# Last layer of a graph network: where a tile's second normalisation stands in VectorE's instruction order

## The reference

```python
def _L0_gnn_ref(...):
    h = x @ W_in + b_in
    for l in range(4):
        h_scaled = h * dinv
        msg = segment_sum(h_scaled[cols], rows) * dinv
        global_ctx = mean(h, axis=0) @ Wg[l] + bg[l]
        z = relu((h + msg) @ Wl[l] + bl[l] + global_ctx)
        mu, var = mean(z, -1), var(z, -1)
        h = (z - mu) * rsqrt(var + EPS) * gamma[l] + beta[l]
    return h

x = x + _L0_gnn_ref(_layernorm(x), src, dst, ...)
x = x + _L0_ffn_ref(_layernorm(x)[None], ...)[0]
```

## Time and profile before

| | |
|---|---|
| three runs, us | 3340.70, 3347.49, 3347.59 (median 3347.49) |
| span of the profiled execution, us | 3340.5 (the page gives no other time for it) |
| TensorE matmul busy | 3129.2 us, 94% |
| TensorE weight load busy | 1810.2 us, 54% |
| VectorE busy | 1989.9 us, 60% |
| ScalarE busy | 850.9 us, 25% |
| GpSimd busy | 70.6 us, 2% |
| products at line 1342 | 9604, 2143.0 us busy |

### The profile page before, as it was taken

The page is one execution under the profiler, slowest core; times in us unless marked ns, Lnnn a source line. Parts: engine busy times, 40 slices in busy tenths (PEclk is TensorE's granted clock), DMA queues, the critical chain, the costliest instruction groups (busy, mean ns, idle before and its releaser), DMA issues.

```text
span 3340.5 us, 56169 instructions
## 1 busy us (share of the span) xinstructions
PE 3129.2 (94%) x17421; PEld 1810.2 (54%) x17421; DVE 1989.9 (60%) x5304; ACT 850.9 (25%) x1934; POOL 70.6 (2%) x168
## 2 busy tenths in 40 slices
PE   6888898699999999999999999999999999979998
PEld 4666676344444444444444444444444444458887
DVE  7999999755455445545554555455555555545554
ACT  3777787411111111111111111111111111123222
POOL 0000000000000000000000000000000000000100
PEclk8999999799999999999999999999999999989999
DMA  4222212412222222221222222221222222110000
GB/s 133 79 79 79 71 49 79 115 68 75 69 67 70 74 68 67 68 76 67 67 76 69 67 67 73 72 67 67 77 78 69 76 78 74 62 34 19 17 17 19
DMA packets 134136, 225.44 MB, mean 67 GB/s; under 512 B 12277, under 2 KB 106596, under 8 KB 134018
## 3 DMA queue, kind: packets, MB, share of 16 engines
q1 hardware_dynamic: 131666, 217.53, 20.2%
q0 software_dynamic: 2352, 6.40, 0.7%
HBM read 178.17 MB, written 45.74 MB: 67 GB/s over the span
## 4 chain that ended last, share of the span: by engine, by line
PE 80%; DVE 11%; issue 4%; ACT 2%; DVEq 1%; DMA 1%; SPq 0%; ACTq 0%; POOL 0%; POOLq 0%
PE bank L1342 50%; PE bank L1212 9%; PE bank L1416 5%; PE bank L1422 5%; PE bank L1300 4%; PE bank L1230 2%; PE bank L1198 2%; PE bank L1290 2%; PE bank L1228 1%; PE bank L1236 1%; DMA tab<-in_x 1%; DVE region L865 1%; DVE region L858 1%; DVE st L870 1%; DVE region L878 1%
## 5 line engine op out<-in xcount | busy, mean ns | idle before, releaser
L1342 PE MATMUL bank<-tab,region 128*128 128x512 f16 x9604 | 2143.0, 379 | 11.4 <-DMA region<-adjacency 11.2
L1342 PEld LDWEIGHTS bank<-tab,region 128*128 128x128 fp8e4 x9604 | 940.3, 98 | 1063.0 <-DVE tab L790 17.1
L1212 PE MATMUL bank<-region 128*128 128x320 bf16 x1862 | 316.4, 320 | 49.8 <-DVE region L670 48.3
L670 DVE TENSOR_SCALAR region<-iota_w,src_col,src_w 128x640 bf16<-128x640 int16 x931 | 361.0, 437 | 0.0
L865 DVE SCALAR_TENSOR_TENSOR region<-bank,c_back,bias 128x256 f32<-128x256 f32 x196 | 94.8, 483 | 405.7 <-PE bank L1300 405.7
L1029 ACT ACTIVATE tab<-region 128x640 fp8e4<-128x640 uint8 x490 | 307.2, 712 | 18.5 <-DVE region L701 18.5
L1212 PEld LDWEIGHTS bank<-region 128*128 128x128 f16 x1862 | 232.6, 144 | 124.4 <-DVE region L670 95.7
L1127 ACT ACTIVATE sd<-mv,eps_c 128x1 f32<-128x1 f32 x196 | 57.8, 295 | 820.8 <-DVE mv L872 820.8
L862 DVE TENSOR_TENSOR region<-bank,region 128x256 f16<-128x256 f32 x196 | 83.2, 425 | 297.6 <-ACT region L1125 297.6
L1125 ACT ACTIVATE region<-bank 128x256 f16<-128x256 f32 x196 | 75.3, 384 | 594.9 <-PE bank L1290 594.9
L1416 PE MATMUL bank<-tab 128*128 128x384 f32 (+1 forms) x544 | 177.2, 484 | 2.6 <-DMA b_s<-in_L_ffn_b 2.6
(11 more groups left out here) (194 smaller groups left out, 2143.9 us busy)
## 6 DMA issues: line engine op xcount, KB each, us to landing
region<-adjacency SPq DMA_DIRECT2D x196, 784.0 KB, 4.3
adjacency<-tab SPq DMA_DIRECT2D x12, 3136.0 KB, 13.9
region<-in_x POOLq DMA_DIRECT2D x48, 128.0 KB, 2.3
out<-region SPq DMA_DIRECT2D x48, 128.0 KB, 1.7
tab<-in_x SPq DMA_DIRECT2D x1, 6016.0 KB
tab<-in_L_ffn_W SPq DMA_DIRECT2D x4, 512.0 KB, 4.2
Wg_s<-in_L_gnn_Wg SPq DMA_DIRECT2D x1, 1024.0 KB
region<-in_L_gnn_Wl SPq DMA_DIRECT2D x1, 1024.0 KB, 5.6
```

What stands on the lines that cost most here:

```text
L670: ins = v.tensor_scalar(hot_s[:, j, :], iota_w[:], src_col[:, ds(start + j, 1)], src_w[:, ds(start + j, 1)], ALU.is_equal, ALU.mult)
L1212: ins = mm(bank[k % 2 * 2 + half][:, 0:HALF], hot_d[:, :, j], hot_s[:, j, half * HALF:(half + 1) * HALF], start=j == 0, stop=j == WIN - 1)
L1342: ins = mm(acc[a][:, :], A_s[:, a, m, :], tab[:, here + m, :], start=m == 0, stop=m == T - 1)
```

## The change

Two helpers are cut out of the last layer's tile on VectorE, `moments(t)` (lines 892 to 897 of the kernel before) and `normal(t)` (lines 898 to 905), and one on ScalarE, `spread(t)` (lines 1131 and 1132). For each of the 48 tiles of the loop in the last layer, `moments` of the tile before now stands between `U` and the split, `normal` of the tile before between the split and the wait for the weight product, and on ScalarE `spread` of the tile before between the copy of the transpose and the square root of the layer's own normalisation. For the last tile all three stand behind the loop. `normal` writes its product to `Zg` instead of `Z`. The other layers are unchanged.

```diff
+            def moments(t):
+                end_own.at(t * CE)
+                hold(dve, x1_ready, t + RING + 1)
+                end_own.done(v.bn_stats(st[:], H[:, t, :]))
+                end_own.hold()
+                end_own.done(v.bn_aggr(mv2[:], st[:]))
+                end_own.wait()
+                v.tensor_copy(mv_all[:, t, :], mv2[:]).then_inc(var2_ready, 1)
+
+            def normal(t):
+                end_own.at(t * CE + 2)
+                dve.wait_ge(std2_ready, t + 1)
+                end_own.done(v.reciprocal(rstd_all[:, ds(t, 1)], sd2[:]))
+                end_own.wait()
+                end_own.done(v.tensor_scalar(Zg, H[:, t, :], mv_all[:, t, 0:1], rstd_all[:, ds(t, 1)],
+                                             ALU.subtract, ALU.mult))
+                end_own.wait()
+                add_rows(t, Zg).then_inc(xsum, 1)
...
+                    late = last and a < RING
+                    if late:
+                        moments(t - 1)
                     dve.wait_ge(uT_copied, n + 2)
                     v.tensor_tensor(uT[:, 1, :, :], T3[3], uT[:, 0, :, :], ALU.subtract).then_inc(uT_split, 1)
+                    if late:
+                        normal(t - 1)
 
                     dve.wait_ge(mm_done, n + 1)
...
                     v.tensor_tensor(H[:, t, :], hf, xb[:, u, :], ALU.add).then_inc(x1_ready, 1)
-                    hold(dve, x1_ready, t + RING + 1)
-                    end_own.done(v.bn_stats(st[:], H[:, t, :]))
...
-                    add_rows(t, Z).then_inc(xsum, 1)
                 tiles(dve, step, n0)
+                if last:
+                    moments(T - 1)
+                    normal(T - 1)
...
+            def spread(t):
+                act.wait_ge(var2_ready, t + 1)
+                a.activation(sd2[:], mv_all[:, t, 1:2], ACT.Sqrt, bias=eps_c[:]).then_inc(std2_ready, 1)
...
                     a.activation(uT[:, 0, :, :], T3[3], ACT.Copy).then_inc(uT_copied, 1)
+                    if last and s < RING:
+                        spread(t - 1)
                     act.wait_ge(var_ready, n + 1)
                     a.activation(sd[:], mv[:, 1:2], ACT.Sqrt, bias=eps_c[:]).then_inc(std_ready, 1)
...
-                        act.wait_ge(var2_ready, t + 1)
-                        a.activation(sd2[:], mv_all[:, t, 1:2], ACT.Sqrt, bias=eps_c[:]).then_inc(std2_ready, 1)
```

More of the change, by code:

```diff
@@ L886, in step @@
                         return
-                    end_own.at(t * CE)
                     u = (a + 1) % RING if a < RING else 0
@@ L1129, in step @@
                         high(n, there + t, hf, n + T, h_ready, hi_ready)
-                    else:
-                        act.wait_ge(var2_ready, t + 1)
-                        a.activation(sd2[:], mv_all[:, t, 1:2], ACT.Sqrt, bias=eps_c[:]).then_inc(std2_ready, 1)
                 tiles(act, step, n0)
+                if last:
+                    spread(T - 1)
             layers(act, one)
```

## The result

| | before | after |
|---|---|---|
| runs, median us | 3344.59 (3340.70 to 3347.59, 4 runs) | 3295.55 (3291.18 to 3299.39, 4 runs) |
| ratio, 95% interval | | 0.9858 (0.9846 to 0.9870) |
| profiled execution: span, time | 3340.5 | 3297.5, 3299.24 |

What follows compares the result with a forecast made beforehand. The prediction took a loop through VectorE and TensorE to bound the last layer at 12.46 us a tile, against TensorE's 11.45. Gains of 47.5 + 1.4 = 48.9 us gave 3347.5 - 48.9 = 3298.6 us, range 3289 to 3311.

Steps and rivals of the forecast that it cites:

- The circle of 12.35 to 12.46 us: Last layer's loop through VectorE and TensorE, line 865 to `U` to weight product, said to set the pace per tile.
- with 1.8 us to spare: Last layer: with 2.84 us moved out, the loop falls to 9.6 us, below TensorE's own 11.45 us.
- Moments hidden between `U` and split, scaling behind it: Last layer's VectorE gaps: moved steps of 1.14 and 1.22 us cost 0, leaving 0.6 and 0.5 us.
- Cadence or idle rows: Last layer's 47 periods: gain taken as 47.5 us from transpose starts, not 37.4 us from TensorE's idle.
- The rival with 0.06: Last layer: only TensorE's shown idle comes back, gain 38.8 us, time 3308.7 us; chance 0.06.
- the missing 0.2 us: Per tile of the last layer, the difference between the gain by transpose starts and by TensorE's idle rows.
- The last tile: Behind the last layer's loop: `U` and the final transpose come sooner, gain 1.4 us, bounds 1.0 and 1.5.
- the 1.27 us worked out: Last tile: `U` ends 1.27 us earlier, by layer 2's 1.94 us from the start of ScalarE's copy.
- the last tile's own residual steps: Behind the last tile: these steps stand there as before, so their change was put at 0.
- From span to median: Whole kernel: the median's 7.0 us above the profiled span was carried over, from 3291.6 to 3298.6 us.

Runs made afterwards that it cites:

- e2: Kernel before with the transpose after 20 sums instead of 14 and the weight product after 30 instead of 24; 3352.9 us.
- e3: Kernel before with six sums instead of ten between the transpose and the weight product, VectorE's and ScalarE's lists untouched; 3299.4 us.
- e6: Changed kernel with eight unused 128x256 adds on VectorE per tile of the last layer, right behind the residual; 3333.8 us.
- e7: Changed kernel with moments, scaling and row sum all between `U` and the split; 3310.5 us.
- e1: Kernel before with only scaling and row sum moved behind the next tile's split, moments and square root left at the tile's end; 3292.3 us.
- e4: Changed kernel with moments, scaling and row sum all behind the split, none between `U` and the split; 3294.1 us.
- e9: Changed kernel with unused TensorE products: 8 ahead of the row sum, 22 ahead of the weights' spread, 12 ahead of the first expert weights; 3294.6 us.
- e8: Changed kernel with unused TensorE products: 26 ahead of the row sum, 20 ahead of the expert weights' spread; 3295.9 us.

## Why the prediction was right

*What bounds the last layer.* The circle of 12.35 to 12.46 us held in every test: not moved by giving `U` more time (e2), shortened as computed on the other arc (e3), lengthened by more work (e6, where 12.5 to 13.1 us were expected and 12.23 came, since the eight adds took 2.68 us and not 2.8 to 3.4, and the loop without them is 9.55 us).

*After the change TensorE is the bound, with 1.8 us to spare.* Cadence 11.449 us, predicted 11.45. The reserve is 11.45 - 9.55 = 1.9 us by e6.

*Moments hidden between `U` and split, scaling behind it.* Both as computed, with more left over than I had said: 0.77 and 0.94 us where I gave 0.6 and 0.5. Two causes: VectorE begins the moments at 2630.69, before `U`'s instruction has ended (2630.77), and the square root is back before it is asked for.

*Cadence or idle rows.* I took 47.5 us against the 37.4 us of the idle rows, and 47.5 us came. The rival with 0.06 would have been 3308.7. The reason that the prediction gave for the missing 0.2 us, a transpose that begins before the sums in front of it are marked as ended, is right for 0.16 of it: e3 and e7 lose 0.17 and 0.34 us a tile where the idle rows of the products show 0 and 0.18. The rest is the longer start of a transpose that has waited, 0.06 us, which the prediction didn't have. The Trainium skill's remark that a matmul's end is computed and not seen (Perfetto Trace Analysis, Tensor Engine Instruction) fits this: the time is really lost, and the computed end hides it.

*The last tile was the term of wrong size.* I took 1.4 us with bounds 1.0 and 1.5; it is 2.2. It has three parts. The final transpose is 12.25 - 10.64 = 1.6 us sooner: ScalarE's copy starts 0.35 us sooner without the square root in front of it, where I allowed 0.2, and the rest is the 1.27 us worked out. From transpose to line 865 it is 3.22 us before and 2.97 after, since the two products of the transpose take 0.44 us instead of 0.69. The granted clock fits this: before, it was already at 0.50 during the transpose; after, it was at 1.00 during the transpose and fell behind it, to 0.70 in the mean (busy times from the transpose to the weight product, before and after):

```profile
2940.09:2941.72 1.63, 0.69 (x3) 0.30 (x3) 0.42 (x1) 0.38 (x1) 0.00 (x0) 0.50 0.00 0
```

```profile
2894.16:2895.53 1.37, 0.44 (x2) 0.20 (x3) 1.06 (x4) 0.68 (x2) 0.00 (x0) 0.70 0.00 0
```

TensorE had been idle for 3.60 us in front of that transpose before and for 2.05 after. Third, the last tile's own residual steps are faster, which I had put at 0: from the residual to the row sum's end it was 2950.41 - 2947.09 = 3.32 us and is 2903.85 - 2900.91 = 2.94 us, now that they stand behind the loop, with fixed addresses and wait values. The two row sums, before and after:

```profile
2949.93 0.48 DVE L795 SCALAR_TENSOR_TENSOR hsum<-region,valid,hsum 128x256 f32<-128x256 f32 x1
```

```profile
2903.36 0.49 DVE L795 SCALAR_TENSOR_TENSOR hsum<-region,valid,hsum 128x256 f32<-128x256 f32 x1
```

Standing behind the loop is what makes the difference: in e1, where moments and square root of the last tile stay in the loop's code and only scaling and row sum stand behind it, the same steps take 2898.66 - 2895.51 = 3.15 us, about half of the way; in e4, with all of them behind it, 2.94. That the fixed values are the reason is argued from the lists, not tested alone.

*From span to median.* I carried the 7.0 us between span and median over. The median of before came out at 3344.6 with one more run, 2.9 us lower, and that of after 3.0 us under the forecast.

*What was luck.* That the medians lie 49.0 us apart where 48.9 were forecast. The two stages that the change touches gained 47.53 + 2.25 = 49.8 us, the spans of the two profiles differ by 43.0, and the four runs of the kernel after lie up to 8.2 us apart. The interval of the ratio allows a gain of 43 to 52 us. What was forecast by its mechanism and came is the cadence, 11.449 for 11.45 us.

## What to carry to other kernels

When two engines hand a tile back and forth, read the distance between starts of one instruction, compare it with a stage in which the suspected engine never waits, and add up the loop: it can set the pace even when every engine in it is idle part of the time (before) or seems to be never idle (e3). Work that nobody in the loop waits for belongs in the gaps of the loop, and only as much must leave it as brings it below the next bound; past that, the exact place cost nothing here while the loop ran, unless it stood in front of what the bound engine needs next (e7), and under 1 us once behind the last tile (e1, e4). A shorter arc on either engine does the same, so look for the cheapest one: here two numbers in TensorE's order (e3) were worth 40 of the 49 us.

## What the runs showed of the hardware

The idle rows of TensorE's products understate a wait. A run of 128x512 sums is marked as 0.16 us longer than the time to the next start (8.58 against 8.42 us for 39 sums, kernel after), and a wait of that length has no row; e3 lost 0.17 us a tile without one, e7 0.34 us with one of 0.18. The rows of the weight loads did show the wait of e3. A transpose that had waited kept the next sum off for 0.28 us instead of 0.22 (e3). Independent adds of 128x256 on VectorE, shown as 0.42 us long, start 2.68 / 8 = 0.335 us apart when none waits for another (e6). TensorE's clock was at its lower level from the router to the first experts; unused products in all three waits raised it and took 2.5 us off the 32 products behind (e9). Too many in front of the router delayed it by 3.8 us, and with the last wait left unfilled the 32 products took 13.20 us as before (e8).
